# A decoder layer on one core: where the context's keys and values are made, the banks of the tail, and the ranks of the dense lists

## The reference

```python
h = x + mamba(rmsnorm(x, norm1_w))            # in_proj, conv of 4 taps, silu, selective scan, silu(z), out_proj
xn = rmsnorm(h, norm2_w)
a = h + (silu(xn @ w1.T) * (xn @ w2.T)) @ w3.T
x = layernorm(x + a)
K = ctx @ Wk.T + bk;  V = ctx @ Wv.T + bv     # per batch: 64 keys, 16 heads of 32
qk = Q @ K.T                                  # per head, Q from x
t = exp(mlp(mean(qk), mean(max(qk)), mean(var(softmax(qk)))))   # one temperature per batch and head
x = layernorm(x + (softmax(qk / (2 * t)) @ V) @ Wo.T + bo)
x = layernorm(x + x @ W.T + b + low_rank_mixture(x))            # top 2 of 8 experts, rank 16
```

## Time and profile before

| | us |
|---|---|
| median of 3 runs | 4237.48 (4236.95 to 4242.27) |
| the profiled execution | 4236.39 |
| its span, first to last instruction | 4234.6 |
| TensorE busy | 3678.8 (87%) |
| VectorE busy | 2507.1 (59%) |
| GpSimd busy | 2491.3 (59%) |
| ScalarE busy | 2173.1 (51%) |

### The profile page before, as it was taken

One profiled execution on the slowest core, in us unless ns is written; L12 is line 12 of the kernel. 1 busy time (PEld: TensorE's weight loads), 2 busy tenths in 40 slices (PEclk: granted clock), 3 DMA queues, 4 the chain that ended last, 5 costly groups with the idle time before them and its releaser, 6 DMA issues.

```text
span 4234.6 us, 36098 instructions
## 1 busy us (share of the span) xinstructions
PE 3678.8 (87%) x9848; PEld 1746.2 (41%) x9848; DVE 2507.1 (59%) x3319; ACT 2173.1 (51%) x5186; POOL 2491.3 (59%) x1100
## 2 busy tenths in 40 slices
PE   6555999799979998999989998999989999999577
PEld 3111433343434345554334335554334435554254
DVE  2676378747774886248774786347774787322211
ACT  3453445554565556455556457365556457341543
POOL 0999199819982996119981997209990998200000
PEclk9555999899989998999989999999989999999788
DMA  4333245324433452125442443225442443112000
GB/s 151 109 115 112 84 159 161 128 93 152 165 123 105 151 167 97 63 75 179 157 134 79 160 159 115 70 61 171 156 138 79 151 162 132 55 55 80 10 30 20
DMA packets 221267, 483.17 MB, mean 114 GB/s; under 512 B 31884, under 2 KB 32268, under 8 KB 220812
## 3 DMA queue, kind: packets, MB, share of 16 engines
q1 hardware_dynamic: 221068, 480.87, 34.8%
HBM read 470.82 MB, written 9.96 MB: 114 GB/s over the span
## 4 chain that ended last, share of the span: by engine, by line
PE 44%; POOL 5%; DVE 5%; ACT 5%; issue 3%; POOLq 0%; ACTq 0%; DVEq 0%
PE ps L1490 24%; PE ps L1579 4%; PE ps L1591 4%; POOL hb L961 4%; PE ps L1548 3%; DVE hb L1296 2%; PE ps L1624 2%; POOL hb L951 2%; PE ps L1658 1%; PE ps L1670 1%; ACT ps L1171 1%; PE ps L1687 1%; PE ps L1700 1%; PE ps L1541 1%; PE ps L1651 1%
## 5 line engine op out<-in xcount | busy, mean ns | idle before, releaser
L951 POOL TENSOR_TENSOR hb<-dtu,bc 128x1024 f32<-128x1024 f32 x512 | 1206.4, 2358 | 114.1 <-PE ps L1591 77.8
L961 POOL TENSOR_TENSOR hb<-hb,bc 128x1024 f32<-128x1024 f32 x512 | 1206.7, 2357 | 97.0 <-issue 45.8
L1490 PE MATMUL ps<-fT,wden 128*128 128x512 f32 x2304 | 1037.9, 598 | 17.5 <-DVE hm L1334 6.0
L1010 ACT ACTIVATE ps<-dt,a_neg 128x512 f32<-128x512 f32 x1024 | 691.3, 689 | 641.1 <-DVE hb L1296 635.6
L1591 PE MATMUL ps<-hb,ident 128*128 128x512 f32 x1024 | 621.1, 698 | 277.5 <-POOL hb L961 275.1
L1490 PEld LDWEIGHTS ps<-fT,wden 128*128 128x128 f32 x2304 | 438.4, 192 | 572.5 <-issue 569.2
L1296 DVE TENSOR_TENSOR_SCAN hb<-ps,state,hb 128x512 f32<-128x512 f32 x512 | 626.7, 1266 | 34.8 <-ACT ps L1010 21.7
L1296 DVE TENSOR_TENSOR_SCAN hb<-ps,hb 128x512 f32<-128x512 f32 x512 | 595.8, 1205 | 16.0 <-POOL hb L951 10.6
L1305 DVE TENSOR_TENSOR ps<-ps,hb 128x512 f32<-128x512 f32 x512 | 355.6, 695 | 377.2 <-POOL hb L961 376.1
L1579 PE MATMUL ps<-wden,hm 128*128 128x512 f32 x1024 | 478.2, 613 | 13.8 <-DVE res L1350 10.2
L1490 PE MATMUL ps<-xnT,wmix 128*128 128x512 f32 x1024 | 464.3, 603 | 10.1 <-ACT xnT L1034 7.8
(11 more groups left out here) (193 smaller groups left out, 3891.7 us busy)
## 6 DMA issues: line engine op xcount, KB each, us to landing
bc<-bc_dram SPq DMA_DIRECT2D x1024, 256.0 KB, 3.5
wden<-in_w SPq DMA_DIRECT2D x192, 512.0 KB, 3.6
wmix<-in_w_mix SPq DMA_DIRECT2D x96, 512.0 KB, 3.6
watt<-in_w_qof SPq DMA_DIRECT2D x32, 512.0 KB, 4.4
xm<-in_x SPq DMA_DIRECT2D x8, 1024.0 KB, 5.3
res<-in_x SPq DMA_DIRECT2D x8, 1024.0 KB, 6.6
wden<-in_w_qof SPq DMA_DIRECT2D x16, 512.0 KB, 3.9
out<-res SPq DMA_DIRECT2D x8, 1024.0 KB, 4.4
```

What stands on the lines that cost most here:

```text
L951: TTn(hb[:, k % 4], dtu[:, :, :], bc[:, 0, k % 3].unsqueeze(1).broadcast_to([P, 2, CH]), ALU.mult).then_inc(s.s1_ready, 1)
L961: TTn(hb[:, k % 4], hb[:, k % 4], bc[:, 1, k % 3].unsqueeze(1).broadcast_to([P, 2, CH]), ALU.mult).then_inc(s.s3_done, 1)
L1010: A_(dst, dt[:, p % 2, jj], ACT.Exp, scale=a_neg[:, j, n:n + 1]).then_inc(full_of(key), 1)
L1490: ins = M(dst, a, b, start=start and n == 0, stop=stop and n == len(pairs) - 1)
```

## The change

The keys and values become units of list `y` (`key`, `value`), ahead of everything else in it, which may run once `proj` of chunk 0 is done. Their inputs go to memory that is free then (`xw`, `res`, `hm`), the results to `qT`. SyncE loads x first, then the constants, then three blocks of mixer weights, then the context. The stores and the loads of batches 0 and 1 become entries of `LOADS`. When chunk 7's `turn_out` is done, the planner gives the mixer's four banks to the other lists. `PHASE` has a number for each chunk instead of one for even and one for odd, `LOOK` has other numbers, and in the planner's picture of a step the exponentials and the scan are two halves each, as they are in the program.

```diff
 def y_plan():
-    got = []
+    got = [("key", 0, c4) for c4 in range(KC)] + [("value", 0, b) for b in range(BATCH)]
...
-            part(ACT_, 1.35, ("scan", c, k - 1), ("sp4", c, 2 * (k // NS) + 1), name=("exp", c, k))
+            for jj in range(2):
+                part(ACT_, 0.68, ("scan", c, k - 1, jj), ("sp4", c, 2 * (k // NS) + 1), name=("exp", c, k, jj))
...
-        part(DVE, 2.5, ("s1", c, i), ("exp", c, i), name=("scan", c, i))
+        for jj in range(2):
+            part(DVE, 1.25, ("s1", c, i), ("exp", c, i, jj), name=("scan", c, i, jj))
...
+    if kind == "key":
+        part(PE, 2 * MM, ("proj", 0), takes=(u,))
+        part(ACT_, 0.5, mine(), gives=(u,))
+    elif kind == "value":
+        part(PE, 4 * MM, ("proj", 0), takes=(u,))
+        part(DVE, EV, mine(), gives=(u,))
...
-PHASE = {"y": (6.12, 6.26), "s": (7.49, 7.0), "x": (9.46, 7.8)}
+PHASE = {'y': (6.888, 6.145, 6.243, 6.145, 6.168, 6.188, 5.839, 6.17), 's': (7.11, 6.999, 7.458, 6.999, 7.49, 6.664, 7.274, 6.744), 'x': (9.747, 7.507, 9.914, 7.263, 8.957, 7.091, 9.431, 7.112)}
...
+            if u == ("turn_out", CHUNKS - 1):
+                free.update({k: end for k in RING_F})
...
-LOOK = {"m": 0.25, "l": 0.1, "x": 0.09, "y": 0.3, "s": 0.3}
+LOOK = {'m': 0.177, 'l': 0.091, 'x': 0.049, 'y': 0.3, 's': 0.3}
...
-    for b in range(1, BATCH):
-        got.append((DONE[("woa", 2 * b - 3, TT - 1)] + 1 if b > 1 else 1.0, 2, ("kv_load", b)))
+    kept = DONE[("value", 0, BATCH - 1)]
+    got += [(kept, 2, ("kv_store", 0)), (kept + 4, 2, ("kv_load", 0)), (kept + 5, 2, ("kv_load", 1))]
+    for b in range(2, BATCH):
+        got.append((DONE[("woa", 2 * b - 3, TT - 1)] + 1, 2, ("kv_load", b)))
...
+            def store_kv():
+                for c4 in range(KC):
+                    emptied(sp, ("key", 0, c4))
+                for b in range(BATCH):
+                    emptied(sp, ("value", 0, b))
+                for c4 in range(KC):
+                    sp.dma_start(k_dram[:, c4].rearrange("b p k -> p b k"), kT[:, c4].rearrange("p (b k) -> p b k", b=BATCH)
+                                 ).then_inc(s.kv_stored, 16)
+                for b in range(BATCH):
+                    sp.dma_start(v_dram[b], vR[:, b]).then_inc(s.kv_stored, 16)
+                sp.wait_ge(s.kv_stored, 16 * 2 * BATCH)
...
-            dve.wait_ge(s.kv_stored, 16 * 2 * BATCH)
```

More of the change, by code:

```diff
@@ L269, in parts @@
     elif kind == "sc1":
-        part(PE, TURN, ("query", c, last), ("kv", b), takes=(u,))
+        part(PE, TURN, ("query", c, last), ("kv", b), ("value", 0, BATCH - 1), takes=(u,))
     elif kind == "mx":
@@ L399, in schedule @@
             share[name][u[1]] = share[name].get(u[1], 0.0) + sum(p[1] for p in got)
[L400 removed]
+            key = 0 if name == "m" else 1 if name == "l" else u[1] + PHASE[name][u[1]] + share[name][u[1]] / WORK[name]
             by_eng = {}
@@ L868, in load_kv @@
                                  ).then_inc(kv_in[r], 16)
[L871 to L879, removed]
@@ new lines, in _ @@
+            load_x(0)
+            for dst, src in ((ident[:, :], A["identity"]), (e64[:, :], A["e64"]), (w_ra[:, :, :], A["w_ra"]),
+                             (w_b[:, :], A["w_b"]), (w_dt[:, :], A["w_dt"]), (cols[:, :], A["cols"]),
+                             (a_neg[:, :, :], A["a_log"]), (t_w1[:, :], A["t_w1"]), (t_w2[:, 0:HID], A["t_w2"]),
+                             (t_w3c[:, :], A["t_w3"]), (t_b[0:HID, 0:1], A["t_b1"]), (t_b[0:HID, 1:2], A["t_b2"]),
+                             (t_b[:, 2:3], A["t_b3"].partition_broadcast(P)), (f_sc[:, :], A["f_sc"])):
+                sp.dma_start(dst, src).then_inc(s.const_in, 16)
@@ L886, in _ @@
-            load_kv(0)
             for unit in LOADS:
@@ L994, in _ @@
             A_(ln1[:, :], zero3[:, 0:1], ACT.Ln, bias=ones_t[:, 0:1]).then_inc(s.act_consts, 1)
-            for c4 in range(KC):
-                act.wait_ge(s.kv_full, c4 + 1)
-                A_(hbf[:, 1024 + c4 * 256:1024 + c4 * 256 + 256], ps[:, c4, 0:256], ACT.Identity,
-                   bias=bk_c[:, c4:c4 + 1]).then_inc(s.kv_out, 1)
             act.wait_ge(s.act_consts, 2)
@@ L1115, in _ @@
                         A_(fT[:, c4], filled(act, key), ACT.Copy, scale=norm2[:, c4:c4 + 1]).then_inc(free_of(key), 1)
+                elif kind == "key":
+                    A_(kT[:, i], filled(act, unit)[:, 0:BATCH * KEYS], ACT.Identity, bias=bk_c[:, i:i + 1]).then_inc(free_of(unit), 1)
                 elif kind == "hg":
                     src = filled(act, ("h1", c, i))
+                    if c == 0 and i == 1:
+                        emptied(act, ("value", 0, BATCH - 1))
                     if i >= FG:
@@ L1152, in _ @@
                 elif kind == "query":
+                    if c == 0 and i == 0:
+                        act.wait_ge(s.kv_stored, 16 * 2 * BATCH)
                     if c > 1 and i == 0:
@@ L1240, in _ @@
             V.tensor_scalar(conv_w, conv_w, 0.5, None, ALU.mult).then_inc(s.dve_consts, 1)
-            dve.wait_ge(s.ctx_in, 64)
-            for b in range(BATCH):
-                dve.wait_ge(s.kv_full, KC + b + 1)
-                V.tensor_tensor(hbf[0:KEYS, 2048 + b * 512:2048 + b * 512 + 512], ps[0:KEYS, 4 + b], spt[0:KEYS, 0, :],
-                                ALU.add).then_inc(s.v_out, 1)
             dve.wait_ge(s.act_consts, 2)
@@ L1329, in _ @@
                     V.reciprocal(smo[:, 2, :], smo[:, 1, :]).then_inc(s.rstd2_ready, 1)
+                elif kind == "value":
+                    V.tensor_tensor(vR[:, i], filled(dve, unit)[0:KEYS], hm[0:KEYS, 1], ALU.add).then_inc(free_of(unit), 1)
                 elif kind == "hg":
@@ L1560, in _ @@
                         ins.then_inc(full_of(key), 1)
+                elif kind in ("key", "value"):
+                    pe.wait_ge(s.ctx_in, 64)
+                    dst = take(pe, unit)
+                    wi = res[:, 1 + (kind == "value")]
+                    if kind == "key":
+                        ins = group(dst[:, 0:BATCH * KEYS], [(wi[:, ci, i * P:(i + 1) * P], ctxT[:, ci]) for ci in range(KC)])
+                    else:
+                        ins = group(dst[0:KEYS], [(ctxT[:, ci, i * KEYS:(i + 1) * KEYS], wi[:, ci]) for ci in range(KC)])
+                    ins.then_inc(full_of(unit), 1)
                 elif kind in ("h", "hv"):
```

39 lines of the change are left out of this document (13 added, 26 removed).

## The result

| | before | changed |
|---|---|---|
| median of the runs, us | 4237.22 (4231.54 to 4242.27, 4 runs) | 4203.31 (4199.21 to 4209.08, 4 runs) |
| profiled execution, us | 4236.39 | 4199.21 (span 4197.4) |

The ratio is 0.9921, 95% interval 0.9903 to 0.994. The time lies in the range given (4164 to 4213), but the gain is 34 us where 51 were forecast, and 4203 is outside the forecast's own 4174 to 4198. The range held only because it reached over rival 1 (4207: the ranks bring nothing), and that is nearly where the time is.

A forecast was written before the change was run, and what follows sets the result against it. Bounds in turn: the opening, GpSimd in recurrences 0 to 2, TensorE from chunk 3 to chunk 7's SwiGLU. Terms -36.8 + 0 + 9 - 21 - 3 = -51.8 took 4236.4 to 4184.6, median 4186; range 4164 to 4213.

The forecast's parts named there:

- rival 1: Odd chunks' recurrences: the ranks bring nothing, as GpSimd's waits grow elsewhere; 4207, or 4210 with Term 5 at zero; chance 0.30.
- Term 1: Opening: with x loaded first, ScalarE's squares of x start at 12.7 instead of 49.55, 36.8 us earlier.
- Term 2: Chunk 0's front: the keys' and values' matmuls fit TensorE's idle time before z 0; cost 0, worst case 2.9 us.
- Term 3: Chunk 0's recurrence: stores and loads on SyncE's queue delay rows of B for GpSimd at steps 5 and 6; cost 9 us.
- rival 4: Whole kernel: chunk 0's gain is taken back later, since TensorE bounds from chunk 3 on; 4237, chance 0.04.
- rival 5: Chunks 2, 5 and 7: moved normalization delays the query and the next turn_in, making the kernel slower; 4252, chance 0.04.
- Term 4: End of recurrences 3, 5 and 7: new ranks fill TensorE's idle time with SwiGLU, gaining 7 us each, 21 together.
- Rival 2: End of odd chunks' recurrences: the ranks bring more because TensorE's clock comes back too; 4162, chance 0.12.
- Term 5: Tail: four more banks bring 0, but chunk 6's last statistics standing earlier gain 3 us of a 9.2 wait.
- The forecast's sign: Chunk 7's statistics: ScalarE still waits 1.36 us before each maximum.
- rival 3: Tail: banks were missing after all, TensorE's 11.6 us of waits for the statistics' sums come back; 4174, chance 0.05.

The follow-up runs named there:

- e4_spread: Changed kernel with the stores and loads of keys and values issued one by one, 4.7 us apart, over chunk 0's recurrence: 4199.62 us, ratio to before 0.9919.
- e5_dose: Changed kernel with twelve further loads behind the second load of keys and values on SyncE's queue: 4219.65 us in one run.
- after_again: The changed kernel run once more, unchanged: 4209.82 us, ratio to before 0.9939.
- e2_ranks: The kernel before with only the new ranks, look-ahead and planner's parts, without the move and the banks: 4238.82 us, ratio to before 1.0016.
- e6_swap: Changed kernel with eight of sixteen exponentials moved behind the softplus on ScalarE in chunks 3, 5 and 7: 4223.74 us, ratio to before 0.9976.
- e3_nobanks: Changed kernel without the four more banks in the tail: 4209.97 us, ratio to before 0.9946.
- the third group: The third set of runs, on one chip beside the kernel before; the changed kernel took 4209.82 us there.
- e7_early: Changed kernel with ten of the fourteen constants loaded later, behind the mixer's weights: 4205.45 us, ratio to before 0.994.

## Why: the prediction step by step

**Term 1 (36.8) was right.** Squares at 13.27 against 12.7 forecast, 36.3 earlier; the first product at 74.87 against 74.7.

**Term 2 (0) was 1.** GpSimd's fifth product waits 1.21 for sum 0, between the two ends named (0 and 2.9); the taken value was at the lower end. e4_spread keeps this wait, so it is the matmuls, not the queue.

**Term 3 (9) was 6.8,** at the place and from the cause stated, shown from both sides by e4_spread (gone) and e5_dose (7.0 more of issuing, 8.3 more of stall). Stall one was 3.00 for 4.8: GpSimd came 1.3 later, nearly all of it from term 2, which the sum counted apart, and the row of B had landed 0.5 earlier than worked out. The second, 3.77, lies in its 2.6 to 5.3. The sentence on the Trainium skill (DMA: Bandwidth & Descriptors, Specifications: pieces of at least 512 B for line rate) took the 8.0 to landing of the earlier trace rows for a sign of small pieces. The same loads with the same pieces land in 2.3 and 2.6 here, with no weights ahead of them in the queue. So the pieces don't explain the 8.0, and the 4.5 that I hung on it didn't come: the row of B behind these loads landed 3.6 after its issue. What line rate such pieces reach, no run here shows.

Terms 1 to 3 together: chunk 0's recurrence ends 28.9 earlier (27.8 forecast; 27.0 in after_again), and the move alone makes the whole 28 to 29 faster. It passes on whole, and rival 4 falls. That the sum is this close is in part luck: term 2 was 1.2 too low and term 3 was 2.2 too high. Of rival 5 there is no sign: chunk 4's first product comes 27.5 earlier than before, chunk 6's 35.9.

**Term 4 (-21) is the step that failed.** It read the idle time of the last sixth as a gap that any dense work fills, and priced the move at 7 a chunk. The dense work does fill it (8, 6 and 7), but it is taken from an earlier place, where it had covered the round trip for `dt`. Over a whole odd chunk, from its first product to the next chunk's (for the last, to `turn_out`), TensorE's idle time is 39.1, 37.8 and 29.5, against 37.4, 36.1 and 28.3 before (for chunk 3: 529.9 less 490.8 busy, and 535.1 less 497.7). That chunk 3 is 5 shorter all the same is not the ranks': the four kernels with the move and the old ranks take 528.4 to 532.7. Rival 2's clock comes back in the last sixth and is lost in the fourth. The larger loss is one that the term never looked at, chunk 2: from its first product to chunk 3's the nine profiles with the new ranks take 422.0 to 425.6, the five with the old ones 416.4 to 418.4, with or without the move and the banks. Which unit of the new order makes TensorE wait there stays open. e2_ranks shows +7 us in all for ranks, look-ahead and parts (interval 3 to 11). The prediction had no gain as its lower bound and as rival 1, a loss only in rival 5, and for another reason; rival 1 got less chance than it deserved, since the place from which the filler comes was never looked at. It also said that VectorE's and ScalarE's fine timing is hidden under GpSimd's fixed 4.7; in the fourth sixth GpSimd is busy for 49.32 of 58.20. What exactly holds the round trip is only half settled: e6_swap shows that the exponentials alone don't, and that TensorE's `dt` group ends within 1.5 of them. Putting that group earlier on TensorE wasn't tried.

**Term 5 (-3) was -5 to -6.** The statistics' order is worth what was taken: behind the last `w3`, e3_nobanks takes 295.3 against 298.8, 3.5 less, and the wait of 9.2 is 7.3. The forecast's sign held, 1.35 before each maximum. The banks were put at 0 on the argument that TensorE is busy for 174.48 of 175.00. That window began at 3750, and of the 1.8 of waiting 1.3 lay ahead of it. The 6.8 us at the low clock lay inside, behind 3757; they are the 0.98 in the row, which the argument passed over: a full engine at half clock counts as busy. With the banks the waiting is gone and the dense stretch takes 203.0 to 204.7 against 208.2 to 209.0. The shortest of them has no low clock, but after_again, with the same banks, has a clock of 0.99 there and takes 1.7 longer, so the part that is the clock's isn't shown to be the banks'. In the statistics rival 3's reason was wrong and the objection right: the 11.6 moves on into the wait for `sta`.

**The sum by what was measured:** -36.7 + 1.2 + 6.8 = -28.7 for chunk 0, about +7 for the ranks, which includes 2 to 3 gained in the tail by their order, and -2 to -5 for the banks: -24 to -27. The changed kernel measured -34 in its own runs and -26 in the third group. The terms can't be told apart further than that by medians: an interval is 0.3% wide, 13 us. So 7 to 10 of the 34 stay unexplained; they lie within that width.

## What to carry to other kernels

Before idle time is priced as fillable, ask which place the filler is taken from and what latency it covers there; sum the idle time over both, and over every other stage whose order changes, as the even chunk did here. A queue that a block of issues occupies costs its issue time as soon as the reserve of loads behind it is used up; spread one per step, the same issues cost nothing here. When a wait ends near two releasers, removing one shows little: look for what ends next before moving work.

## What the runs showed of the hardware

Two profiles of the same program, same order on every engine, lie 9.9 us apart (4197.4 and 4207.3), more than most of the terms argued about. It comes in steps, of which the largest, 5.5, lies between the first products of chunks 5 and 6 and comes with TensorE's granted clock. From chunk 6's `turn_in` to its first product, first profile and second:

```profile
2736.80:2821.70 84.90, 78.09 (x284) 43.57 (x284) 42.25 (x85) 55.36 (x155) 2.35 (x1) 0.94 0.24 76
```

```profile
2740.90:2830.20 89.30, 82.49 (x284) 47.94 (x284) 42.24 (x85) 55.35 (x155) 2.40 (x2) 0.89 0.24 72
```

The same 284 matmuls, 4.4 longer at 0.89 of the clock instead of 0.94, while VectorE and ScalarE did the same work in the same time. Other steps are not the clock's: 1.3 in the opening, 0.6 in the second wait for a row of B, and 3.2 more of TensorE's idle time in chunk 1. A difference of a few us between two profiles behind a TensorE-bound stretch is no evidence, and one of 1 to 2 isn't even in front of it (chunk 0). The differences that stand here are those that repeat in several kernels: the two waits of chunk 0, chunk 2's stage, the fourth and last sixths, the tail. The landing time of a load also isn't one number: the keys' 32 KB took 2.3 here and 8.0 before, behind x and six weight loads in the queue. The 4.8 of e7_early and the 2.4 of the changed kernel can't be compared as sizes: `w_dt` is 512 KB behind the 1 MB of x, the last constant is a few bytes.
